# Flags, rank and maximum ahead of the normalising burst; first load and last stores in halves; weights prepared ahead of step 0

## What is computed

```python
x = x + box3x3(ln_c(x))                 # LayerNorm over the 256 channels of each pixel, then a 3x3 mean per channel
t = to_tokens(x)                        # one token of 256 values per pixel
n = ln_t(t)                             # LayerNorm of each token
a_lo = argmax(n[..., 16:32] > 0.5);  a_hi = argmax(n[..., 32:48] > 0.5)
b_lo = argmax(n[..., 48:64] > 0.5);  b_hi = argmax(n[..., 32:48] > 0.5)
# flags of columns 0..2 select "add", "sub" or nothing; columns 65 and 66 are two more features
y = mlp(features, Wa, ba) if add, mlp(features, Ws, bs) if sub   # three layers of 80, ReLU between them
# result nibbles -> one-hot added to columns 64..79 and 72..87, carry to column 80
out = from_tokens(t + (n with those additions))
```

## Time and profile before

| | us |
|---|---|
| median of 3 runs | 703.15 |
| lowest, highest | 701.91, 705.96 |
| the profiled execution, its time | 703.77 |
| its span in the profile | 702.0 |

### The profile page before, as it was taken

How to read it: one execution, slowest core, us unless ns; L and a number is a source line. 1 busy time by engine, 2 the same in 40 slices (tenths; PEclk the granted TensorE clock), 3 DMA queues, 4 the chain that set the end, 5 groups by cost and what they waited for, 6 DMA issues and landing times. The chain is left out here.

```text
span 702.0 us, 10740 instructions
## 1 busy us (share of the span) xinstructions
PE 530.0 (76%) x2254; PEld 237.7 (34%) x2294; DVE 588.0 (84%) x1414; ACT 487.9 (70%) x739; POOL 315.0 (45%) x580
## 2 busy tenths in 40 slices
PE   0034789888888898878888889879888888998860
PEld 0011234343333343433333334434333333443320
DVE  1579989999999999969999999879999999995130
ACT  0112589877778877767777887768777778788820
POOL 0123556554455455535445555544554455554000
PEclk9997799999999999989999999979999999999995
DMA  9999992697459907991479926910459039296999
GB/s 107 109 158 186 194 183 40 81 167 113 61 92 166 165 15 107 150 183 28 60 107 166 147 30 91 167 15 0 60 68 112 0 52 94 19 89 44 88 84 74
DMA packets 625656, 67.96 MB, mean 97 GB/s; under 512 B 625472, under 2 KB 625600, under 8 KB 625600
## 3 DMA queue, kind: packets, MB, share of 16 engines
q1 hardware_dynamic: 624496, 67.29, 83.8%
q10 hardware_dynamic: 1104, 0.13, 0.2%
HBM read 33.86 MB, written 33.55 MB: 96 GB/s over the span
## 5 line engine op out<-in xcount | busy, mean ns | idle before, releaser
L801 ACT ACTIVATE xbuf<-xbuf,shift,gain (+1 forms) x256 | 223.6, 944 | 0.0
L647 POOL TENSOR_TENSOR nlo<-n,nhi 128x1024 f16<-128x1024 f32 x64 | 167.2, 2614 | 123.4 <-ACT nhi L783 123.4
L531 DVE BATCH_NORM_STATS2 stat<-xbuf 128x6 f32 (+1 forms) x256 | 171.4, 682 | 20.4 <-DMA xbuf<-x 20.3
L878 PE MATMUL ps<-h1m,w2m 128*128 128x512 f32 x256 | 136.5, 615 | 24.8 <-ACT h L770 20.9
L522 DVE TENSOR_SCALAR n<-xbuf,stat,rns 128x256 f32 (+1 forms) x256 | 134.9, 602 | 1.3
L880 PE MATMUL ps<-h1r,w2r 128*128 128x512 f32 x256 | 133.3, 603 | 0.0
L783 ACT ACTIVATE nhi<-n 128x1024 f16<-128x1024 f32 x64 | 67.9, 1061 | 93.6 <-DVE n L522 93.6
L841 PE MATMUL ps<-nhi,band 128*128 128x512 f16 (+1 forms) x408 | 107.8, 378 | 16.3 <-POOL nlo L647 14.6
L841 PE MATMUL ps<-nlo,band 128*128 128x512 f16 (+1 forms) x408 | 106.2, 373 | 0.0
L549 DVE TENSOR_TENSOR xbuf<-ps,xbuf 128x512 f32 (+1 forms) x128 | 91.6, 716 | 11.2 <-PE ps L841 9.3
L657 POOL TENSOR_TENSOR ut<-xbuf,stat 128x16 f32<-128x16 f32 x32 | 7.2, 225 | 190.1 <-DVE shift L450 190.1
(11 more groups left out here) (87 smaller groups left out, 575.7 us busy)
## 6 DMA issues: line engine op xcount, KB each, us to landing
xbuf<-x SPq DMA_DIRECT2D x16, 1024.0 KB, 11.4
out<-xbuf SPq DMA_DIRECT2D x32, 512.0 KB, 7.1
xbuf<-x SPq DMA_DIRECT2D x30, 512.0 KB, 7.0
out<-xbuf SPq DMA_DIRECT2D x12, 1024.0 KB, 12.8
out<-xbuf SPq DMA_DIRECT2D x16, 256.0 KB, 7.9
xbuf<-x SPq DMA_DIRECT2D x4, 256.0 KB, 8.2
consts<-cst SPq DMA_DIRECT2D x1, 171.0 KB, 2.4
h<-ws ACTq DMA_DIRECT2D x4, 10.0 KB
```

Source lines behind the costliest of these rows:

```text
L531: return v.bn_stats(stat[:, j % 4, at + 2 * s:at + 2 * s + 2, :].rearrange("p w n -> p (w n)"), xview(par)[:, w:w + 2, :].rearrange("p w c ...
L647: pool.tensor_tensor(nlo[:, at:at + HALF, :], n32[:, h, :, :], nhi[:, at:at + HALF, :], ALU.subtract).then_inc(lo_ready, 1)
L801: ins = act.activation(col, col, ACT.Identity, bias=shift[:, k, w:w + 1], scale=gain[:, k, w:w + 1])
L878: pe.matmul(ps[:, B_L2, :], w2m[:, :], h1m[:, i % 2, :], start=True, stop=False)
```

## The change

- `compare`, `rank` and `top` move ahead of the burst `normalise(0..7)` in every step on DVE, and stand directly one behind another. `put(0)` and `put(1)` move forward by one place each: `put(0)` ahead of the second statistics of x1, `put(1)` ahead of the last statistics of x.
- The first load is the whole first half (32 columns); step 0 waits for it. `FIRST_PART` and `first_loaded` are gone.
- `setup_parts` and `setup_weights` stand ahead of step 0 on DVE, and `setup_weights` with the wait for its end ahead of step 0 on PE.
- The last pair is stored in two halves.

```diff
-FIRST_PART = W // 4
-LAST_PARTS = (0, W // 4, W // 2, 3 * W // 4, W)
+LAST_PARTS = (0, W // 2, W)
...
             sp.dma_start(cst[:, :], cst_d).then_inc(cst_loaded, 16)
-            load(0, 0, (0, C), (0, FIRST_PART), first_loaded)
...
-                        start = FIRST_PART if pair == 0 and h == 0 else h * HALF_W
-                        load(pair, pair, chans, (start, (h + 1) * HALF_W), x_loaded[h])
+                        load(pair, pair, chans, (h * HALF_W, (h + 1) * HALF_W), x_loaded[h])
...
-                if known(t) and t == 2:
-                    setup_parts()
-                if known(t) and t == 3:
-                    setup_weights()
                 finish(0)
-                if known(t) and t == 0:
-                    v.wait_ge(first_loaded, 16 * IMGS)
-                elif first:
-                    half = {(FIRST_PART // CW if known(t) else 0): 0, CHUNKS // HALVES: 1}.get(j)
+                if first:
+                    half = {0: 0, CHUNKS // HALVES: 1}.get(j)
...
                 finish(5)
+                compare()
+                rank()
+                top()
                 for w in range(CW):
                     normalise(w)
-                compare()
                 add_convolution(1)
-                rank()
                 x_statistics(2)
                 wait_x1(1)
-                top()
+                put(0)
                 x1_statistics(1)
                 add_convolution(2)
-                put(0)
+                put(1)
                 counted = x_statistics(3)
-                put(1)
                 wait_x1(2)
...
+            setup_parts()
+            setup_weights()
             run_steps(v, step)
...
-                if known(t) and t == 2:
-                    setup_weights()
-                if known(t) and t == 4:
-                    pe.wait_ge(setup_v, SETUP_V)
...
+            setup_weights()
+            pe.wait_ge(setup_v, SETUP_V)
             run_steps(pe, step)
```

More of the change, by code:

```diff
@@ L226, in build @@
         setup_pe = sem("setup_pe")
-        first_loaded = sem("first_loaded")
         x_loaded = [sem(f"x_loaded{h}") for h in range(HALVES)]
```

## The result

| | us |
|---|---|
| before, median in the same comparison (12 runs) | 702.69 |
| after, median (12 runs) | 706.7 |
| after, lowest and highest | 702.22, 709.55 |
| ratio after / before, 95% interval | 1.0059, 1.0042 to 1.0076 |
| span of the profiled execution, after | 705.2 |

The forecast was 697 us and faster; the changed kernel is slower by 0.6%, which is just more than this kernel's measurement can tell from no change. The range of 688 to 707 holds the time, at its upper end.

The account below looks back on a forecast made before the run. DVE, busy 84%, was taken to bound the kernel, with ACT's chain next at 18.9 us per step. From 703.77, loop +8.5, start -3.9 and end -11.2 gave 697.2; forecast 697 us, about 694 to 701, rivals 688 to 707.

Parts of the forecast that it names:

- the term of the loop: 24 loop steps: +4.6 us for steps of 19.1 us and +4 for delayed bursts, taken as +8.5.
- steps 3 to 7: Steps ahead of the loop: about 2.4 us lost, up to 1.9 each in steps 5 and 6.
- The start: First load and setup: later landing +1.7, setup moved ahead saves time; -3.9 us in all, bounds -6.5 and -1.
- rival 3: Start: weights land behind the x stream at 25 us, setup costs its 7 us in full; 703 us, chance 0.07.
- The end: Last stores: only one late range of 1.05 MB stands behind DVE's last instruction; -11.2 us, bounds -6 and -12.
- rival 4: Last stores: the early half still runs at 682.6 and half the gain is lost; 703 us, chance 0.08.
- gw and yy: DVE instructions in the loop, blocked behind POOL: would run free, 1.31 and 0.42 us less per step.
- ACT's ring: Loop chain reciprocal, nhi, ACT's stream, square root, reciprocal: from 17.0 to 18.9 us, as the burst starts 1.88 later.
- caught bursts: Loop: in four of 24 steps nlo gets the lock inside the burst; 1.0 us each, +4 us, bounds 0 and 8.
- The dead heat: Loop, behind the burst: POOL's second nlo at 3.99 us against ym at 4.05; who gets the lock left open.
- rival 1: Loop: POOL wins the lock from ym each time, steps of 19.6 us, +16.8; median 707 us, chance 0.15.
- the block: Loop: ym or hot waits behind POOL's second nlo, 1.4 to 2.1 us; DVE's path 18.8 to 19.6 us.

Follow-up runs that it names:

- c1_ends: The kernel before with only the last pair stored in two halves: 692.73 us, ratio 0.985.
- v2: Kernel before, both edges changed, two-SBUF-input instructions clear of POOL's rests, last two one-hot additions behind the variance; compare, rank, top ahead of the burst: 701.87 us.
- m1_ym: The changed kernel with ym (put(3)) one place earlier, ahead of the statistics of x1: 700.15 us, ratio 0.996.
- v4_fill: The changed kernel with ten unused matmuls in each loop step where PE waits for the ReLU h: 702.42 us, ratio 1.000.
- c4_edges: The kernel before with the new first load, setup and last stores, but the old order of a step: 686.07 us, ratio 0.976.
- v3: As v2, but with compare alone ahead of the burst, rank and top behind it: 658.89 us, ratio 0.937.
- c3_order: The kernel before with only the new order of a step on DVE: 722.61 us, ratio 1.026.
- m2_out: The changed kernel with two columns of output moved from ahead of ACT's square root to behind it: 730.42 us, ratio 1.038.

## Why the prediction was wrong, point by point

The sum gave 697.2 us for the profiled execution, which took 707.0. Of the 9.8 us missing, 6.5 are the term of the loop (+8.5 in the sum, +15.0 measured) and 3.1 that of steps 3 to 7 (+2.4 and +5.5). Both come from the path that sets the step.

- **The start held.** First statistics at 25.80 (1.64 later; 1.7 in the sum), the reciprocal of step 3 at 53.58 (53.6). The weights are there at 14.86; rival 3 falls.
- **The end held.** 8.3 us from DVE's last end to the end (8.2 in the sum), and c1_ends gives -10.7 alone; rival 4 falls.
- **gw and yy became free,** 0.36 and 0.18 us, as said. The order's gain on DVE alone is real.
- **ACT's ring was right in size and misused in the sum.** The 18.9 us of the new ring were measured to a tenth in v2, in steps where ACT has no gap. But the step then took "+0.2: the mean of an ACT bound of 18.9 and of DVE at 19.3". A step is as long as the longer of its chains, not their mean. By its own figures the step was 19.3, 0.39 x 24 = +9.4 us, and with the caught bursts +13.4; this is the step that failed. The seventeen undisturbed steps are 19.35 on average. Even so the sum would have been some 702, no change: the five long steps and steps 3 to 7 made it slower.
- **The dead heat was no coin to be tossed for each step.** 3.99 against 4.05 us came out as 379.57 against 379.69: POOL was first in 21 of 24 steps. The same code meets nearly the same distances each time. A tie of 0.06 us should have been priced as rival 1, not as half of it. Rival 1's mechanism is what happened. Its price of 19.6 per step was the size of ten steps (19.45 to 19.80); m1_ym puts the block at 6.5 us of the time, not 16.8. That rival 1's 707 is the time measured is luck.
- **Caught bursts** were taken as four in 24 at 1.0 us each, and there was one, in a step 1.5 us longer than before. Their number changes when the distances around the burst change, so that of before says little about that of after.
- **PE's clock was not in the sum at all.** The prediction treated PE as having slack. It has, but a later `nhi` gathered the slack in one idle of about 2 us in each step. The clock fell in four steps, in two of which it fell before too without a loss, and these four are longer by 5.8 us in all; v4_fill gives back about 4 us.
- **Steps 3 to 7** cost 5.5 us instead of 2.4. They were given "up to 1.9 each" in two steps and room in the others. The steps from 90.04 on are 18.8 long. In the first of them, which took 16.5 before, the ring alone binds (DVE waits 2.28 us for the square root); in the next two DVE's s_var comes 0.2 us behind ACT. The one ahead (19.70, where DVE waits 2.94 us) has a caught burst, as before. m1_ym, without the block, needs 92.05 for the stretch instead of 92.92: the block isn't the main cause.

In short: the prediction had the price of the ring in hand and said itself that DVE's gain can't be had. From there the order could only lose, and everything on top (block, clock, steps 3 to 7) had to be added in full and set against the 17.5 us of the two edges. Without the order the edges give 686.07 (c4_edges).

## What to carry to other kernels

- Of two chains through a step, what is moved ahead of the point where the second chain branches off lengthens it in full, whatever the first one gains. Take the maximum of the chains, not a mean; v2 against v3 is 43 us for 1.25 us more ahead of the burst, of which the longer ring is 29.
- Where two engines reach for one lock within 0.1 us of each other in a loop, take the dear outcome for all turns; here it was enough to move an instruction by one place (m1_ym, 6.5 us).
- Cheap work that must be done but nobody waits for belongs in the wait that ends the step (put(6) and put(7) behind the variance: with it the steps fell from 18.2 to 17.6 us).

## What the runs showed of the hardware

- Between DVE and POOL the earlier starter goes first even when it is ahead by 0.09 to 0.12 us, and this decides whether ym takes 0.20 us or 2.05. In c3_order 0.04 us are enough, either way: ym at 428.66 against `nlo` at 428.70 takes 0.15, ym at 447.69 against `nlo` at 447.65 takes 2.13. By the Trainium skill, "SBUF — State Buffer", section "Who interferes with whom", issue order and not the shape of the operation decides who blocks; these rows agree.
- After an idle of 2.15 us, and in m2_out after one of 3.17 us, PE worked at the lower of its two clock levels for some microseconds (pairs of 1.73 to 1.91 us instead of 1.02). The length of one idle doesn't decide it: in the changed kernel it did so after one of 1.92 us (the step at 507.00), and not after 2.15, 2.19 and 2.21 us in three other steps. Matmuls without use in that gap kept the clock up in two steps of the trace, and the kernel became 4 us faster.
- Moving 2 of 8 columns of output to another place of ACT's stream, with no work added, cost 24 us. PE's idle ahead of featT grew and its granted clock fell in 20 of 24 loop steps; how the 24 us divide between the two was not measured.
